# Tiles 6 and 7 of the conditioning matmul computed as a block pair instead of two plain tiles

## The reference, cut to what matters

```python
w_bot = einsum('bg,got->bot', cond_8, weight * mask)      # b=2, g=8, o=t=512
h     = einsum('bnt,bot->bno', x, w_bot) + bias           # x: 2 x 2048 x 512, fp32
# act_quant: scale = 127 / max|row|, round, /scale ; weight_quant: ternary {-1,0,1} / scale
gate  = silu(act_quant(h) @ weight_quant(w_gate).T)       # 512 -> 2048
up    = act_quant(h) @ weight_quant(w_up).T
out   = x + act_quant(gate * up) @ weight_quant(w_down).T # 2048 -> 512
```

## Time and profile before

| | us |
|---|---|
| median of 3 runs | 433.79 |
| the three runs | 433.52, 433.79, 435.25 |
| the profiled execution's own time | 433.37 |
| its span in the trace | 431.6 |
| TensorE busy in the span | 420.2 |
| VectorE, ScalarE, GpSimd busy | 355.1, 305.3, 324.0 |

### The profile page before, as it was taken

The page is one execution under the profiler, slowest core; times in us unless marked ns, Lnnn a source line. Parts: engine busy times, 40 slices in busy tenths (PEclk is TensorE's granted clock), DMA queues, the critical chain, the costliest instruction groups (busy, mean ns, idle before and its releaser), DMA issues.

```text
span 431.6 us, 7666 instructions
## 1 busy us (share of the span) xinstructions
PE 420.2 (97%) x2282; PEld 255.6 (59%) x2282; DVE 355.1 (82%) x593; ACT 305.3 (71%) x459; POOL 324.0 (75%) x306
## 2 busy tenths in 40 slices
PE   4899999999999999999999999999999999999997
PEld 0233588888855465555656556656655655655554
DVE  1236778888897898899999999999999999999891
ACT  1214998788887885877768786777868668786842
POOL 0005999999408999898779796887979779796872
DMA  7999999995213344445555445453354453444766
GB/s 273 404 400 409 295 360 305 306 303 152 59 27 73 62 109 100 134 112 120 102 119 99 133 98 132 110 114 97 97 147 111 108 122 97 111 104 126 114 153 174
DMA packets 104462, 69.84 MB, mean 162 GB/s; under 512 B 87280, under 2 KB 87536, under 8 KB 102896
## 3 DMA queue, kind: packets, MB, share of 16 engines
q1 hardware_dynamic: 103712, 67.13, 57.9%
q10 hardware_dynamic: 720, 2.36, 1.5%
HBM read 40.11 MB, written 8.39 MB: 112 GB/s over the span
## 4 chain that ended last, share of the span: by engine, by line
PE 85%; POOL 9%; DMA 2%; DVE 2%; issue 1%; ACTq 0%; POOLq 0%; DVEq 0%
PE ps L1457 27%; PE ps L1497 18%; PE ps L1577 15%; PE ps L1414 10%; PE ps L1355 7%; PE ps L1404 2%; PE ps L1512 2%; DMA wc<-wcond 2%; PE ps L1368 2%; POOL wc L470 1%; POOL wc L475 1%; POOL wc L473 1%; POOL wc L471 1%; PE ps L1522 1%; POOL gcombo L397 1%
## 5 line engine op out<-in xcount | busy, mean ns | idle before, releaser
L1152 DVE TENSOR_TENSOR wc<-ps,xT_sb 128x512 f32<-128x512 f32 x104 | 69.0, 682 | 5.7 <-issue 2.3
L1497 PE MATMUL ps<-wc 128*128 128x256 f16 x448 | 58.1, 273 | 0.3 <-DVE wc L1105 0.3
L715 ACT ACTIVATE xT_sb<-ps,gate_unit 128x512 f32<-128x512 f32 x78 | 50.5, 685 | 9.2 <-PE ps L1457 8.4
L1186 DVE TENSOR_REDUCE p_part<-wc 128x1 f32<-128x1024 f32 (+2 forms) x42 | 50.9, 1211 | 0.4
L1497 PEld LDWEIGHTS ps<-wc 128*128 128x128 f16 x448 | 43.8, 98 | 12.4 <-issue 0.7
L1414 PE MATMUL ps<-tern_up,qT 128*128 128x512 f16 x192 | 49.3, 379 | 0.0
L486 POOL TENSOR_TENSOR result<-result,x_res 128x512 f32<-128x512 f32 x14 | 18.2, 1301 | 38.1 <-issue 38.1
L1497 PE MATMUL ps<-tern_down,wc 128*128 128x256 f16 x336 | 43.5, 273 | 0.0
L735 ACT ACTIVATE wc<-wc 128x1024 f16<-128x1024 f32 x38 | 39.8, 1051 | 1.6 <-DVE wc L1289 1.2
L1497 PEld LDWEIGHTS ps<-tern_down,wc 128*128 128x128 f16 x336 | 32.9, 98 | 12.8
L720 ACT ACTIVATE wc<-wc,p_scale 128x2048 f32<-128x2048 f32 x18 | 36.0, 2001 | 5.7 <-DVE p_scale L1280 5.7
(11 more groups left out here) (164 smaller groups left out, 1047.2 us busy)
## 6 DMA issues: line engine op xcount, KB each, us to landing
xT_sb<-xT SPq DMA_DIRECT2D x32, 256.0 KB, 5.8
x_res<-x SPq DMA_DIRECT2D x30, 256.0 KB, 3.0
out<-result SPq DMA_DIRECT2D x29, 256.0 KB, 2.0
wc<-wcond SPq DMA_DIRECT2D x12, 512.0 KB, 13.3
wc<-w_gate SPq DMA_DIRECT2D x4, 1024.0 KB, 14.7
wc<-w_up SPq DMA_DIRECT2D x4, 1024.0 KB, 8.1
wc<-w_down SPq DMA_DIRECT2D x4, 1024.0 KB, 6.6
wc<-wcond ACTq DMA_DIRECT2D x4, 512.0 KB, 7.7
```

Of the source, the lines that this page charges most:

```text
L715: nc.scalar.activation(gsilu[:, q, i % 2], source, ACT.Silu, scale=unit_column(s + i // 2)).then_inc(gsilu_ready[q], 1)
L1152: nc.vector.tensor_tensor(prod[:, par, 512 * i:512 * i + 512], up, source, ALU.mult).then_inc(prod_ready, 1)
L1186: nc.vector.tensor_reduce(p_part[:, par, i:i + 1], prod[:, par, 512 * lo:512 * hi], AX.X, ALU.max, apply_absolute_value=True).then_inc(par ...
L1497: ins = nc.tensor.matmul(ps[:, bank, cut], tile, weight, start=(i < (2 if apart(j) else 1) and k == 0), stop=(k == KB - 1), skip_group_che ...
```

## The change

- `PLAIN` goes from 8 to 6 and `PAIR0`, the first pair, from 4 to 3: tiles 6 and 7 become pair 3. The loop of plain products for tiles 6 and 7 on TensorE goes.
- Banks: tiles 0 to 5 use banks 4, 5, 0, 1, 2, 3, and pair 3 uses banks 4 and 5.
- GpSimd: the batch 0 combinations are made in eight half size pieces (`combine_cond0`). Four of them, and the four x sums of pair 3, stand ahead of the last quarter's weights, and four behind it. The masking of the batch 1 weights is ordered 3, 0, 1, 2 and has the first sums of pair 4 in its middle.
- ScalarE: `seed_bias(3)` and `copy_first(3)` come in after the first rounding; later copies and absolute sums move against each other.
- VectorE: two `cond_tile` go, and the steps of pair 3 come in; `weight_mean(0)` moves into the loop behind `pair_c22(4)`.
- SyncE: x tiles 8 and 9 are loaded ahead of w_gate piece 2, and x tiles 14 and 15 behind the transposes of tiles 4 and 5. The batch 1 mask pieces come in the order 3, 0, 1, 2.
- TensorE: `abs_total(0)` moves from ahead of product 2 of pair 5 to behind its product 3.

```diff
-PLAIN = 8
-SEEDED = 8
-PAIR0 = SEEDED // 2
+MASK_ORDER = 3, 0, 1, 2
+PLAIN = 6
+PAIR0 = PLAIN // 2
 def cond_bank(t):
-    return t % 8 if t < PLAIN else ...
+    return (t + 4) % 6 if t < PLAIN else ...
...  SyncE
-            for k in range(KH):
+            for k in MASK_ORDER:
                 load_mask(1, k)
             sp.wait_ge(mix_psum, 4)
+            load_xT(8)
+            load_xT(9)
             load_raw(0, w_gate, 2)
-            for t in range(8, 12):
-                load_xT(t)
+            load_xT(10)
+            load_xT(11)
...
-            load_xT(14)
-            load_xT(15)
             load_raw(1, w_up, 1)
             transpose_q(4)
             transpose_q(5)
+            load_xT(14)
+            load_xT(15)
...  GpSimd
+            def combine_cond0(i, k):
+                pool.wait_ge(w_bot0_ready, KH if i == 3 else k + (1 if i == 0 else 3))
+                b11, b12 = w_bot[:, 0, k, 0:NB], w_bot[:, 0, k, NB:HID]
+                b21, b22 = w_bot[:, 0, 2 + k, 0:NB], w_bot[:, 0, 2 + k, NB:HID]
+                if i in (1, 3):
+                    pool.wait_ge(cond_t_ready[0], (0, 2, 0, 6)[i])
+                in0, in1 = ((b12, b11), (b22, cond_t0[:, 0, k]), (b22, b12), (b21, cond_t0[:, 1, k]))[i]
+                nc.gpsimd.tensor_tensor(cond_t0[:, i, k], in0, in1, ALU.subtract).then_inc(cond_t_ready[0], 1)
-            combine_cond(0)
-            for k in range(KH):
+            for k in range(2):
+                combine_cond0(0, k)
+            combine_cond0(2, 0)
+            combine_cond0(1, 0)
+            first_sums(3)
+            last_sums(3)
+            combine_cond0(2, 1)
+            combine_cond0(1, 1)
+            for k in range(2):
+                combine_cond0(3, k)
+            for k in MASK_ORDER[:2]:
                 apply_mask(k)
             first_sums(4)
+            for k in MASK_ORDER[2:]:
+                apply_mask(k)
             last_sums(4)
...  ScalarE
             cond_round(0)
+            seed_bias(3)
+            abs_sum_piece(0, 1)
+            copy_first(3)
             seed_bias(4)
-            abs_sum_piece(0, 1)
             cond_round(1)
+            cond_round(2)
+            copy_first(4)
+            cond_round(3)
             seed_bias(5)
-            cond_round(2)
-            cond_round(3)
-            abs_sum_piece(0, 2)
-            copy_first(4)
             cond_round(4)
             cond_round(5)
+            abs_sum_piece(0, 2)
+            copy_first(5)
             abs_sum_piece(0, 3)
-            copy_first(5)
...  VectorE
-            for t in range(PLAIN - 1):
+            for t in range(PLAIN - 2):
+                cond_tile(t)
+            pair_share(3)
+            pair_seed(3)
+            for t in range(PLAIN - 2, PLAIN):
                 cond_tile(t)
             pair_share(4)
-            pair_seed(4)
-            cond_tile(PLAIN - 1)
-            pair_share(5)
-            pair_c22(4)
-            weight_mean(0)
+            pair_c22(3)
...  TensorE
                 if i == 0:
-                    pe.wait_ge(cond_t_ready[b], 4)
+                    pe.wait_ge(cond_t_ready[b], (8, 4)[b])
                     pe.wait_ge(x_sum_ready, 4 * n + 1)
-                    pe.wait_ge(h_ready, 7)
+                    if n == 0:
+                        pe.wait_ge(half_copied, 2 * KH)
-            for t in range(EARLY, SEEDED):
-                ...
-                cond_products(t, range(KH))
+                pair_product(r, 2)
+                pair_product(r, 3)
                 if r == 5:
                     abs_total(0)
-                pair_product(r, 2)
-                pair_product(r, 3)
```

More of the change, by code:

```diff
@@ L54, in cond_bank @@
 def cond_bank(t):
-    return t % 8 if t < PLAIN else 2 + t % 2 if t >= LATE else 2 * ((t // 2 - 7) % 3) + t % 2
+    return (t + 4) % 6 if t < PLAIN else 2 + t % 2 if t >= LATE else 2 * ((t // 2 - 7) % 3) + t % 2
 def apart(j):
@@ L320, in _ @@
             load_xT(19)
-            for r in range(PLAIN // 2, PAIR_END):
+            for r in range(4, PAIR_END):
                 for t in (2 * r, 2 * r + 1):
@@ L399, in combine_gate @@
                     nc.gpsimd.tensor_tensor(combos[:, 3, k], b21, combos[:, 1, k], ALU.subtract).then_inc(done, 1)
-            def combine_cond(b):
[L402 to L407, removed]
+            def combine_cond0(i, k):
[6 more added lines that the diff above has]
+                nc.gpsimd.tensor_tensor(cond_t0[:, i, k], in0, in1, ALU.subtract).then_inc(cond_t_ready[0], 1)
+            def combine_cond(b):
+                b11, b12 = w_bot[:, 1, 0:2, 0:NB], w_bot[:, 1, 0:2, NB:HID]
+                b21, b22 = w_bot[:, 1, 2:4, 0:NB], w_bot[:, 1, 2:4, NB:HID]
+                done = cond_t_ready[1]
+                pool.wait_ge(w_bot1_ready, KH)
+                nc.gpsimd.tensor_tensor(cond_t[:, 0], b12, b11, ALU.subtract).then_inc(done, 1)
+                nc.gpsimd.tensor_tensor(cond_t[:, 2], b22, b12, ALU.subtract).then_inc(done, 1)
                 pool.wait_ge(done, 1)
-                nc.gpsimd.tensor_tensor(combos[:, 1], b22, combos[:, 0], ALU.subtract).then_inc(done, 1)
+                nc.gpsimd.tensor_tensor(cond_t[:, 1], b22, cond_t[:, 0], ALU.subtract).then_inc(done, 1)
                 pool.wait_ge(done, 3)
-                nc.gpsimd.tensor_tensor(combos[:, 3], b21, combos[:, 1], ALU.subtract).then_inc(done, 1)
+                nc.gpsimd.tensor_tensor(cond_t[:, 3], b21, cond_t[:, 1], ALU.subtract).then_inc(done, 1)
             def apply_mask(k):
@@ L638, in seed_bias @@
                 if r < PAIR0 + 3:
-                    act.wait_ge(h_ready, 2 * r - 6)
+                    act.wait_ge(h_ready, 2 * r - 4)
                 else:
@@ L913, in _ @@
             cond_round(0)
+            seed_bias(3)
+            abs_sum_piece(0, 1)
+            copy_first(3)
             seed_bias(4)
-            abs_sum_piece(0, 1)
             cond_round(1)
+            cond_round(2)
+            copy_first(4)
+            cond_round(3)
             seed_bias(5)
-            cond_round(2)
-            cond_round(3)
-            abs_sum_piece(0, 2)
-            copy_first(4)
             cond_round(4)
             cond_round(5)
+            abs_sum_piece(0, 2)
+            copy_first(5)
             abs_sum_piece(0, 3)
-            copy_first(5)
[L926 to L929, removed]
             for r in range(PAIR0 + 2, PAIR_END):
-                copy_first(r)
+                if r > PAIR0 + 3:
+                    copy_first(r)
                 pair_round(r - 2, 1)
@@ L935, in _ @@
                 pair_round(r - 2, 0)
+                if r == PAIR0 + 2:
+                    pair_convert(r - 2)
+                    copy_first(r + 1)
                 if r < 9:
@@ L939, in _ @@
                     abs_sum_piece(2, r - 9)
-                pair_convert(r - 2)
+                if r > PAIR0 + 2:
+                    pair_convert(r - 2)
                 if r >= 13:
@@ L1038, in pair_share @@
                 if r == PAIR0:
-                    dve.wait_ge(w_bot1_ready, KH)
+                    dve.wait_ge(w_bot1_ready, 1)
                 dve.wait_ge(cond_shared, r - PAIR0 + 1)
@@ L1058, in pair_largest @@
                 dve.wait_ge(cond_psum, 2 * r + 2)
-                if r >= PLAIN // 2 + 2:
+                if r >= PAIR0 + 2:
                     dve.wait_ge(h_rounded, 2 * r - 2)
@@ L1310, in _ @@
                 pair_c22(r - 1)
-                if r < 10:
+                if r == 5:
+                    weight_mean(0)
+                elif r < 10:
                     ternary_piece(0, r - 6)
```

## The result

The changed kernel takes 435.35 us (median of 19 runs, 434.87 to 437.43); the kernel before took 433.44 us (19 runs, 432.64 to 435.45). The ratio is 1.0044, with a 95% interval of 1.0032 to 1.0055: slower by 1.9 us, where 0.65 us less was forecast and 434.5 was the upper end of the range. The profiled execution has a span of 433.5 us, against 431.6.

The account below looks back on a forecast made before the run. The prediction took TensorE, busy 97% of the span, as the bound. Removed TensorE work of 0.91 us less a 0.26 us stall saves 0.65 us, giving a median of 433.1 us, with 432.3 to 434.5 as the 8 in 10 range.

Parts of the forecast that it names:

- The gain up to product 1 of pair 6: On TensorE: 0.65 us saved at this point, which should start at about 59.25 instead of 59.92.
- the removed work: On TensorE: plain tiles 6 and 7 (6.96 us) give way to pair 3 (6.05 us), removing 0.91 us.
- the late w_gate piece 2: Rival in SyncE's queue: the piece lands late, TensorE stalls 2.5 us at the sum over partitions, time 435.6; chance 0.12.
- The 0.26 us stall ahead of product 2: TensorE in pair 3: product 2 starts at 45.23, not 44.97, since ScalarE's copy of product 1 ends at 44.94.
- the 0.29 us between a copy's end and the matmul: Read at pair 4: copy ends at 51.64, product 2 starts at 51.93; taken as what a wait needs.
- The lock between the masking and a sum of pair 3: Rival: VectorE and GpSimd share a port, delaying the last quarter's weights; costs 0.02 us, or 0.75 at worst; chance 0.06.
- the one in the sum: After product 1 of pair 6: the other engines wait for TensorE, so the 0.65 us saved reaches the end.
- 3.7 us to spare: GpSimd's four weight pieces behind the last quarter end at about 40.1; TensorE's product 0 wants them at 43.8.
- the move of x tiles 14 and 15: SyncE's queue: they come 3.5 us later, land by 62, wanted at 62 by GpSimd and 65 by TensorE.
- The gain doesn't reach the end: Rival: something later in the kernel is timed by an engine other than TensorE, time 433.8; chance 0.08.

Follow-up runs that it names:

- the own sum buffer: Changed kernel with the x sums of pair 3 in a buffer of their own, the unused qT of tiles 24 to 27: 435.0 us, ratio 1.0034.
- the traces with halved scalings: GpSimd scales only half of each w_gate and w_up piece: 432.88 us in the changed kernel, 433.28 us in the kernel before.
- the run where GpSimd came early: Changed kernel with pair 3's x sums in their own buffer and one more masking ahead of pair 4's first sums: 434.42 us, ratio 1.0025.

## Why the prediction was wrong

**Right.** The gain up to product 1 of pair 6 (0.80 us, where 0.65 was forecast), though by two errors against each other: the removed work is 0.1 us less than the 0.91 (in distances of starts, the 16 plain records are worth 14.69 - 7.83 = 6.86 us and not 6.96), and the stall is smaller. Right also the front of the kernel, where ScalarE, VectorE and the late w_gate piece 2 held nothing up. The 0.26 us stall ahead of product 2 was at most 0.02: of the 0.29 us between a copy's end and the matmul no more than 0.13 are needed (44.13 + 0.36 = 44.49, and the matmul at 44.62). The lock between the masking and a sum of pair 3 happened (0.87 us for 0.69, and 1.17 for 0.73 on GpSimd) and cost nothing, as its rival said; but the rival had the rule at the wrong place.

**The step that failed** is the one in the sum: "From there VectorE, ScalarE and GpSimd are less busy than TensorE and wait for it. Their chains ... start from TensorE's work and so move with it." It was read from GpSimd's busy time of 51.29 in 54.88 us. But 2.3 us at the end of that stretch are a wait for the last products, with nothing else to do. From 72 to 108 us GpSimd is busy 35.14 of 36.00 us, and it waits for no other engine. It does not wait for TensorE; it runs on a lead that shrinks by about 0.1 us in a round. When TensorE comes forward and GpSimd does not, the lead ends, and the engine that had looked hidden is the bound.

**What made it worse than a lost gain.** From product 1 of pair 6 to the first gate product TensorE needs 115.10 - 58.68 = 56.42 us, against 114.76 - 59.92 = 54.84 before: 1.58 lost to rounds of 6.33 us. Then comes product 4 of pair 14, 1.98 us after the gate product instead of 0.86: 1.12 lost to VectorE's operations held up by GpSimd's late sums. Before, these two starts were:

```profile
114.76 1.03 PE L1393 MATMUL ps<-tern_gate,qT 128*128 128x512 f16 x4
115.62 1.03 PE L1577 MATMUL ps<-gcombo,result 128*128 128x256 f32 x4
```

Together 2.70, less the 0.80 gained: 1.90. That the medians (1.91) and the spans (1.9) differ by just as much is in part chance. In the profiled pair the changed kernel began 0.44 us earlier, and about as much is lost behind this point: 0.1 in the next product, 0.05 in the gated network, and 0.3 behind VectorE's last operation, which has 2.5 us to the end of the span for 2.2 before. This last part is in all four runs of the changed kernel without the own sum buffer (2.51 to 2.54 us) and in no other run (2.16 to 2.25); its cause is open. It would also explain why the 0.8 us of the traces with halved scalings are only 0.4 in the medians.

**Where GpSimd's time went.** The prediction priced its waits one by one against TensorE's next product ("3.7 us to spare") and never asked when its next free running stage would start. It also left out a wait that the diff brings without a changed line: with pair 3 ahead of them, the sums of pair 5 are the third user of two buffers. And the move of x tiles 14 and 15 was costed against a GpSimd that arrives late; it used up the margin that a faster one would need (a wait of 1.76 us in the run where GpSimd came early).

**The chances.** "The gain doesn't reach the end" had 0.08, and at 433.8 its price had only one direction. An engine that becomes the bound was not among the rivals as slower than before, though the shared port, which the prediction has as a rival for another place, and GpSimd's timeline were both at hand.

## What to carry to other kernels

An engine that is off the chain but has no waits of its own is a second bound with a lead, and the lead is a number to be read: the distance between when its product is ready and when it is used, and how much that shrinks per round. A change that moves the first engine forward has to move this one as well; here 0.8 us of less TensorE work cost 1.9 us until GpSimd's buffer, its order and three pairs of x tiles in the DMA queue had been changed with it.

Where two engines hold each other up, the length of a round depends on their phase, so a delay of 1.3 us can cost 2.7. Read the durations of the same instruction in several rounds (0.73, 1.18, 1.72): they say which phase the kernel is in.

## What the runs showed of the hardware that was not expected

- The same GpSimd sum (128x256 fp32) takes 0.73 us alone, and 0.99 to 1.73 us beside a VectorE conversion; the same VectorE conversion (128x2048) takes 1.22 to 1.74 us beside GpSimd. In the one phase a round of the two is 6.15 us, in the other 6.33 us, and each held for seven rounds (the short one in the run with tiles 18 and 19 moved, the long one in the changed kernel).
- VectorE operations on 16 columns took 0.70 us beside GpSimd sums of 0.73 to 1.17 us, instead of 0.23: a small operation can be held up for most of a whole one of the other engine.
- Under one program the kernel's time has two values 2 us apart (432.0 to 433.1, and 434.2 to 435.2 with tiles 16 and 17 moved once). That the landing of one DMA decides between them is likely, and not shown.
